# A graph network kernel: count matrices from steps of 256 edges instead of 128, and pair locations as bytes

## The reference: what is computed

```
# layer 0
h_proj = einsum('nd,rde->rne', h, relation_weight)
att = sum(h_proj[etype, src] * tanh(h_proj[etype, dst] + efeat), axis=-1)
a = softmax of att over the edges of each dst
h_nb = segment_sum(h[src] * a[:, None], dst)
# layer 1, four times
x = segment_sum(dinv[src] * dinv[dst] * x[src], dst)
# layer 2: gated convolution over (x[dst], x[src], edge_attr); layer 3: two attention layers
```

## Time and profile before

| | before |
|---|---|
| median of 3 runs | 9190.53 us (9164.67 to 9205.76) |
| the profiled execution | 9157.66 us, span 9156.1 us |
| mean granted TensorE clock | 0.608 |
| busy in the span | PE 3846.7 us (42%), DVE 5285.9 (58%), ACT 2454.3 (27%), POOL 3780.2 (41%) |
| count tiles' loads (tile<-adj) | 228 of 781.2 KB |
| x_src<-rows_s, window<-hpx in relation_rows | stores of 896 KB, loads of 256 KB |

### The profile page before, as it was taken

How to read it: one execution, slowest core, us unless ns; L and a number is a source line. 1 busy time by engine, 2 the same in 40 slices (tenths; PEclk the granted TensorE clock), 3 DMA queues, 4 the chain that set the end, 5 groups by cost and what they waited for, 6 DMA issues and landing times. The chain is left out here.

```text
span 9156.1 us, 102588 instructions
## 1 busy us (share of the span) xinstructions
PE 3846.7 (42%) x24601; PEld 3085.2 (34%) x24602; DVE 5285.9 (58%) x8989; ACT 2454.3 (27%) x3870; POOL 3780.2 (41%) x4315
## 2 busy tenths in 40 slices
PE   5455555520017881444443232222249522222196
PEld 2444444520017881333333210000048300000186
DVE  5454445569742112444444468888856588888675
ACT  4333333321622221433333221111112111111121
POOL 4444444400020004444444236666625166666261
PEclk8555555555558995666666555555579555555596
DMA  7565556677737881222222366666645477666462
GB/s 291 152 186 174 170 179 186 184 212 194 284 67 266 293 281 52 82 83 80 93 80 81 44 179 183 184 183 184 171 99 132 128 183 185 182 183 183 107 139 69
DMA packets 1551900, 1462.17 MB, mean 160 GB/s; under 512 B 1296593, under 2 KB 1344365, under 8 KB 1535296
## 3 DMA queue, kind: packets, MB, share of 16 engines
q1 hardware_dynamic: 966152, 807.40, 28.8%
q0 software_dynamic: 175712, 462.09, 19.3%
q10 hardware_dynamic: 409944, 191.70, 7.4%
HBM read 1078.30 MB, written 381.40 MB: 159 GB/s over the span
## 5 line engine op out<-in xcount | busy, mean ns | idle before, releaser
L2328 POOL DMA_INDIRECT rows_p<-node_rows,stage_i x1728 | 1637.9, 948 | 1090.7 <-issue 842.8
L2359 PE MATMUL psZ<-parts_r,hot_t 126*128 x1728 | 629.5, 468 | 1948.7 <-issue 966.3
L2359 PEld LDWEIGHTS psZ<-parts_r,hot_t 126*128 126x128 bf16 x1728 | 181.0, 105 | 2398.1 <-issue 2378.1
L715 PE MATMUL psP<-window,pair_hot 128*128 x3136 | 725.6, 420 | 579.4 <-issue 349.9
L790 DVE SCALAR_TENSOR_TENSOR pair_run<-pair_run,same_c,psP 128x64 f32<-128x64 f32 x1568 | 440.1, 281 | 871.9 <-remote 743.4
L2416 DVE TENSOR_TENSOR psZ<-psZ,rows_p 128x660 f32<-128x660 f32 x864 | 724.7, 846 | 357.7 <-issue 236.5
L715 PEld LDWEIGHTS psP<-window,pair_hot 128*128 128x128 f32 x3136 | 690.8, 329 | 626.7 <-issue 626.7
L257 POOL DMA_INDIRECT rows_s<-hpx,stage_i x784 | 748.5, 955 | 264.7 <-issue 242.7
L257 POOL DMA_INDIRECT both<-table,stage_i x784 | 742.9, 948 | 264.0 <-issue 242.6
L2423 DVE SCALAR_TENSOR_TENSOR lz<-psZ,att 128x660 f32<-128x660 f32 x864 | 723.0, 837 | 95.1 <-issue 69.1
L2429 DVE TENSOR_REDUCE sc<-lz 128x10 f32<-128x660 f32 x864 | 711.9, 831 | 59.4 <-issue 45.1
(11 more groups left out here) (523 smaller groups left out, 8016.2 us busy)
## 6 DMA issues: line engine op xcount, KB each, us to landing
tile<-adj SPq DMA_DIRECT2D x228, 781.2 KB, 4.8
x_src<-rows_p SPq DMA_DIRECT2D x288, 192.0 KB
xs<-x_src SPq DMA_DIRECT2D x432, 128.0 KB, 3.1
locs<-loc_rows SPq DMA_DIRECT2D x144, 378.0 KB
hpx<-stage ACTq DMA_DIRECT2D x25, 2048.0 KB
pair_loc<-pair_locs SPq DMA_DIRECT2D x28, 1792.0 KB
window<-hpx SPq DMA_DIRECT2D x196, 256.0 KB
dst_runs<-pair_run SPq DMA_DIRECT2D x28, 1792.0 KB
```

Source lines behind the costliest of these rows:

```text
L715: last = pe.matmul(psP[:, n % 2, j * D:(j + 1) * D], hot[:, n % 2, j * CE:(j + 1) * CE], window[:, n % 2, bass.ds(rel[j], 1), :].rearrange ...
L2328: pool.indirect_dma_start(rows[:, k, j, :], None, g.node_rows, bass.IndirectOffsetOnAxis(stage[:, k, j:j + 1], 0)).then_inc(got[k], 16)
L2359: last = pe.matmul(psZ[:, n % 4, j, 0:ZH], hot[:, k, col * CE:(col + 1) * CE], parts[:, bass.ds(at[col], 1), :].rearrange("p o c -> p (o c)"),
```

## The change

- A step is now CS = 256 edges, two chunks side by side (`e` = 0, 1): half as many chunks (CH = 392), fewer steps and NT = 42 tiles. `raw`, `place` and `quo` have 256 elements a step, `colsT` a further axis of 2; 10 rounds with 4 transposes and one copy.
- A step's counts are two matmuls that add in PSUM, each reading every second element of the one-hots. The one-hots of a tile are made in two units, of 12 and 13 steps (both written 13 wide, 6656 elements), with the iota in SBUF in 16 bits, each value twice side by side. The units follow batches 0, 3 and 5 of each chunk (`UNIT_AT`).
- A turn of two chunks makes 3 tiles, 21 parts over 14 batches (one and two in turn), with three tile buffers and a ring of 3 PSUM banks. PE waits for its own products behind both units of a tile. SP stores tiles at n = 2, 7 and 12. No tile is left behind the loops.
- The pair locations go through memory as bytes, one higher than before, and the lanes' number is one lower.

```diff
-CH = EP // CE
+CS = 2 * CE
+CH = EP // CS
 WD = 5
 NW = N // WD
 TS = 25
 TC = TS * WD
-NT = 57
+NT = 42
 S = NT * TS
-SP = 95
+SP = 105
...
+    g.colsT, g.iotaB = g.hot.sb("colsT", [P, 2, 2, S], bf16), g.hot.sb("iotaB", [P, P], bf16)
...
-        keys, locb = t.sb("keys", [CR, PT, CE], i32), t.sb("locb", [CR, PT, CE], bf16)
+        keys, locb = t.sb("keys", [CR, PT, CE], i32), t.sb("locb", [CR, PT, CE], u8)
...
-                        pool.indirect_dma_start(raw[:, n, q, :], None, a[name].rearrange("(c e) -> c e", e=CE),
+                        pool.indirect_dma_start(raw[:, n, q, :], None, a[name].rearrange("(c e) -> c e", e=CS),
...
-                    pe.transpose(psX[:, q % 2, 0:SP], quo[:, q, :], g.ident[0:SP, 0:SP])
-                    pe.transpose(psX[:, q % 2, P:P + SP], place[:, q, :], g.ident[0:SP, 0:SP]).then_inc(cols_turned, 1)
+                    for n, values in enumerate((quo, place)):
+                        for e in range(2):
+                            last = pe.transpose(psX[:, q % 2, (2 * n + e) * SP:(2 * n + e + 1) * SP],
+                                                values[:, q, e * CE:(e + 1) * CE], g.ident[0:SP, 0:SP])
+                    last.then_inc(cols_turned, 1)
...
-                c.link(v.tensor_tensor(locb[:, :, :], keys[:, :, :], pgroup[:, :].unsqueeze(2).to_broadcast([CR, PT, CE]), ALU.subtract))
-                c.link(v.tensor_scalar(locb[:, :, :], locb[:, :, :], -1.0, float(PN * R), ALU.max, ALU.min))
+                c.link(v.tensor_tensor(keys[:, :, :], keys[:, :, :], pgroup[:, :].unsqueeze(2).to_broadcast([CR, PT, CE]), ALU.subtract))
+                c.link(v.tensor_scalar(locb[:, :, :], keys[:, :, :], 0.0, float(PN * R + 1), ALU.max, ALU.min))
...
-                    v.tensor_copy(g.colsT[:, 0, q * SP:(q + 1) * SP], psX[:, q % 2, 0:SP])
-                    v.tensor_copy(g.colsT[:, 1, q * SP:(q + 1) * SP], psX[:, q % 2, P:P + SP]).then_inc(taken, 1)
+                    v.tensor_copy(g.colsT[:, :, :, q * SP:(q + 1) * SP].rearrange("p n e s -> p (n e) s"),
+                                  psX[:, q % 2, 0:4 * SP].rearrange("p (m s) -> p m s", m=4)).then_inc(taken, 1)
...
-    RING = 4
-
-    def __init__(self, nc, g, s):
-        self.nc, self.g = nc, g
-        self.cols = s.sb("cols", [P, 2, 2, TS], bf16)
-        self.hot = s.sb("hot", [P, 2, 2 * TS, P], bf16)
-        self.tile = s.sb("tile", [P, 2, NB, TC], bf16)
-        self.ps, self.iota = s.ps("psA", [P, self.RING, 512]), s.ps("ps_iota", [P, P])
-        self.hot_made, self.hot_used, self.stored = (
-            [s.sem(f"{n}{k}") for k in range(2)] for n in ("hot_made", "hot_used", "tile_stored"))
+    RING = 3
+    FIRST = 3
+    UNITS = (slice(0, FIRST * GS), slice(FIRST * GS, TS))
+    WIDE = TS - FIRST * GS
+
+    def __init__(self, nc, g, s, tiles):
+        self.nc, self.g, self.tiles = nc, g, tiles
+        self.cols = s.sb("cols", [P, 2, 2, self.WIDE, 2], bf16)
+        self.hot = s.sb("hot", [P, 2, 2 * self.WIDE, P, 2], bf16)
+        self.tile = s.sb("tile", [P, tiles, NB, TC], bf16)
+        self.iota = s.sb("iota_w", [P, P, 2], bf16)
+        self.ps = s.ps("psA", [P, self.RING, 512])
+        self.hot_made, self.hot_used = ([s.sem(f"{n}{k}") for k in range(2)] for n in ("hot_made", "hot_used"))
+        self.stored = [s.sem(f"tile_stored{k}") for k in range(tiles)]
         self.counted, self.moved = s.sem("counted"), s.sem("moved")
 
-    def one_hots(self, c, v, tile, k, turn):
-
-
-        v.wait_ge(self.hot_used[k], turn + 1)
-        at = bass.ds(tile * TS, TS) if not isinstance(tile, int) else slice(tile * TS, (tile + 1) * TS)
-        c.link(v.tensor_copy(self.cols[:, k], self.g.colsT[:, :, at]))
-        v.tensor_tensor(self.hot[:, k], self.cols[:, k].rearrange("p n s -> p (n s)").unsqueeze(2).to_broadcast([P, 2 * TS, P]),
-                        self.iota[:, :].unsqueeze(1).to_broadcast([P, 2 * TS, P]), ALU.is_equal).then_inc(self.hot_made[k], 1)
+    def one_hots(self, c, v, tile, k):
+
+
+        v.wait_ge(self.hot_used[k], tile + 1)
+        n, lo = self.UNITS[k].stop - self.UNITS[k].start, self.UNITS[k].start
+        at = bass.ds(tile * TS + lo, n) if not isinstance(tile, int) else slice(tile * TS + lo, tile * TS + lo + n)
+        c.link(v.tensor_copy(self.cols[:, k, :, 0:n, :], self.g.colsT[:, :, :, at].rearrange("p w e s -> p w s e")))
+        v.tensor_tensor(self.hot[:, k], self.cols[:, k].rearrange("p w s e -> p (w s) e").unsqueeze(2).to_broadcast([P, 2 * self.WIDE, P, 2]),
+                        self.iota[:, :, :].unsqueeze(1).to_broadcast([P, 2 * self.WIDE, P, 2]), ALU.is_equal
+                        ).then_inc(self.hot_made[k], 1)
 
     def dve_begin(self, c, v):
-        c.link(v.tensor_copy(self.iota[:, :], self.g.iotaB[:, :]))
+        c.mark(v.memset(self.cols[:, :, :, :, :], -1.0))
+        c.link(v.tensor_copy(self.iota[:, :, :], self.g.iotaB[:, :].unsqueeze(2).to_broadcast([P, P, 2])))
 
     def pe_begin(self, pe):
         for k in range(2):
             pe.sem_inc(self.hot_used[k], 1)
 
-    def products(self, pe, before, r, n, turn):
-
-        NG, GS, k = self.NG, self.GS, r % 2
-        if n == 0:
-            pe.wait_ge(self.hot_made[k], turn + 1)
-        pe.wait_ge(self.moved, before * NG + n + 1)
+    def products(self, pe, i, r, n):
+
+        NG, GS, k, tile = self.NG, self.GS, int(n >= self.FIRST), i * self.tiles + r
+        if n in (0, self.FIRST):
+            pe.wait_ge(self.hot_made[k], tile + 1)
+        pe.wait_ge(self.moved, tile * NG + n + 1)
         for j in range(min(GS, TS - n * GS)):
-            st = n * GS + j
-            last = pe.matmul(self.ps[:, (r * NG + n) % self.RING, j * TC:(j + 1) * TC], self.hot[:, k, st, :],
-                             self.hot[:, k, TS + st, 0:TC], start=True, stop=True)
+            st = n * GS + j - self.UNITS[k].start
+            for e in range(2):
+                last = pe.matmul(self.bank(r, n)[:, j * TC:(j + 1) * TC], self.hot[:, k, st, :, e],
+                                 self.hot[:, k, self.WIDE + st, 0:TC, e], start=e == 0, stop=e == 1)
         last.then_inc(self.counted, 1)
-        if n == NG - 1:
-            pe.wait_ge(self.counted, before * NG + NG)
+        if n in (self.FIRST - 1, NG - 1):
+            pe.wait_ge(self.counted, tile * NG + n + 1)
             pe.sem_inc(self.hot_used[k], 1)
+
+    def bank(self, r, n):
+        return self.ps[:, (r * self.NG + n) % self.RING]
 
     def act_begin(self, act):
         act.sem_inc(self.moved, self.RING)
-        for k in range(2):
+        for k in range(self.tiles):
             act.sem_inc(self.stored[k], 16)
 
-    def move(self, act, before, r, n, turn):
-
-        k, m = r % 2, min(self.GS, TS - n * self.GS)
+    def move(self, act, i, r, n):
+
+        tile, m = i * self.tiles + r, min(self.GS, TS - n * self.GS)
         if n == 0:
-            act.wait_ge(self.stored[k], turn * 16 + 16)
-        act.wait_ge(self.counted, before * self.NG + n + 1)
-        act.activation(self.tile[:, k, :, n * self.GS * WD:(n * self.GS + m) * WD],
-                       self.ps[:, (r * self.NG + n) % self.RING, 0:m * TC].rearrange("p (s a) -> p a s", a=NB),
-                       ACT.Copy).then_inc(self.moved, 1)
-
-    def store(self, sp, before, k):
-
-        sp.wait_ge(self.moved, before * self.NG + (self.NG + self.RING))
-        at = bass.ds(before * P, P) if not isinstance(before, int) else slice(before * P, (before + 1) * P)
-        sp.dma_start(self.g.adj[at, :], self.tile[:, k].rearrange("p a c -> p (a c)")).then_inc(self.stored[k], 16)
-
-    def sp_end(self, sp):
-        sp.wait_ge(self.stored[0], ((NT + 1) // 2 + 1) * 16)
-        sp.wait_ge(self.stored[1], (NT // 2 + 1) * 16)
+            act.wait_ge(self.stored[r], i * 16 + 16)
+        act.wait_ge(self.counted, tile * self.NG + n + 1)
+        act.activation(self.tile[:, r, :, n * self.GS * WD:(n * self.GS + m) * WD],
+                       self.bank(r, n)[:, 0:m * TC].rearrange("p (s a) -> p a s", a=NB), ACT.Copy).then_inc(self.moved, 1)
+
+    def store(self, sp, i, r):
+
+        tile = i * self.tiles + r
+        sp.wait_ge(self.moved, tile * self.NG + (self.NG + self.RING))
+        at = bass.ds(tile * P, P) if not isinstance(tile, int) else slice(tile * P, (tile + 1) * P)
+        sp.dma_start(self.g.adj[at, :], self.tile[:, r].rearrange("p a c -> p (a c)")).then_inc(self.stored[r], 16)
+
+    def sp_end(self, sp, turns):
+        for r in range(self.tiles):
+            sp.wait_ge(self.stored[r], (turns + 1) * 16)
...
-    TB = 4
-    assert M * BP * NCH == NP and 2 * Tiles.NG == 2 * M and TB * (NCH // 2) == NT - 1
+    TB = 3
+    UNIT_AT = {0: (0, 1), 3: (1, 0), 5: (1, 1), 7: (2, 0), 10: (2, 1), 12: (3, 0)}
+    parts_at = [[divmod(q, Tiles.NG) for q in range(TB * Tiles.NG * n // (2 * M), TB * Tiles.NG * (n + 1) // (2 * M))]
+                for n in range(2 * M)]
+    assert M * BP * NCH == NP and TB * (NCH // 2) == NT and TB * Tiles.NG % Tiles.RING == 0
```

(78 more changed lines are left out.)

4 lines of the change are left out of this document (2 added, 2 removed).

## The result

The changed kernel takes 8806 us (median of 4, 8788 to 8855) against 9187 us of the kernel before on the same chip: ratio 0.9595, 95% interval 0.9557 to 0.9634. That is faster by 381 us; forecast were 37 us (9187 or 9190 to 9150), and the range ended at 8985. The profiled execution took 8855.31 us, its span is 8853.0 us, 303 us shorter than the span of before.

The account below looks back on a forecast made before the run. PE bounds propagate; landing, gathers and tail set relation_rows' period. -153 - 5 + 3 + 119 - 4 = -40 us against the profiled 9157.7 gives 9118, or 9150 as a median; range 8985 to 9370.

Parts of the forecast that it names:

- What bounds the kernel: relation_rows chunk: landing some 11 us, gathers 35, tail 13; the crawl is single matmuls with idle between, beside running gathers.
- propagate: Four calls, PE-bound: 57 tiles become 42 in each, 60 fewer at 2.55 us, -153 us.
- Joins: TensorTensors of StepJoins: 1425 elements become 1050, about a dozen save about 0.4 us each, -5 us.
- first_tables: Count columns at its end: 15 rounds become 10 of about 1.1 us with twice the transposes, +3 us.
- One-hot at 3.6 us: relation_rows, DVE: each new 16 bit one-hot takes 3.6 us, 10.9 us a chunk instead of 13.6.
- Rival B: One-hots run no faster, 7.1 us, and hold POOL longer: +12 to +13 us a chunk, 9370 us; chance 0.14.
- One-hots hold POOL: relation_rows: a one-hot with both inputs in SBUF delays POOL's gathers by 0.87 of its length, +3.1 us for one inside.
- How many of them meet the gathers: Of three one-hots a chunk, one at the gathers' start (+1.0 us), one inside (+3.1), one with POOL idle (0).
- Tail (+0.3): From a chunk's last gather to the next store, 13 us: 4 to 8 more matmuls, one ACT move less, +0.3 us.
- rival A: Held gathers let PE catch up, tail 13.1 to about 8 us; chunk -2 to +1, centre 9030 us; chance 0.27.
- Rival C: More count products and PE's own waits lengthen the crawl: +3 to +5 us a chunk, about 9260 us; chance 0.16.
- The sum: Whole kernel: propagate, joins, first_tables, relation_rows chunks (+119 us) and the dropped last tile (-4) make -40 us.

Follow-up runs that it names:

- f1: Changed kernel with its 16 bit iota in PSUM, so one-hots don't hold POOL, on chip 7 with the crawl: 9228 us, 0.997 of the kernel before.
- h1: The changed kernel itself, unedited, measured again on chip 0 with the crawl: 9128 us, 0.979 of the kernel before there.
- a1: The changed kernel itself, unedited, measured again on chip 14 without the crawl: 7665 us, 0.996 of the kernel before there.
- b1: The kernel before itself, unedited, profiled again on chip 14 without the crawl: 7690 us.
- g1: Changed kernel with iota in PSUM and three own POOL stops of 2.4 us in each chunk's gathers, chip 0: 8696 us, 0.933 of before.
- e3: Kernel before with three own POOL stops of 2.4 us in each chunk's gathers, chip 4 without the crawl: 7787 us, 1.012.
- e1: Changed kernel with its 16 bit iota in PSUM instead of SBUF, chip 4 without the crawl: 7490 us, 0.974 of the kernel before.
- g3: Kernel before with six short POOL stops, one behind every fourth gather, each adding 1.15 us, chip 0: 8767 us, 0.941.
- g2: Kernel before with one POOL stop of 2.4 us behind the 14th gather of each chunk, chip 0: 9233 us, 0.991.
- e2: Kernel before with its fp32 iota in SBUF instead of PSUM, chip 4 without the crawl: 7947 us, 1.033.

## Why the prediction was wrong, point by point

- **What bounds the kernel**: right, in the three pieces landing, gathers, tail, and in seeing that the tail is PE's crawl. The tail was read as a fixed 13 us. It depends on how long POOL runs without a stop, and the trace of before had no stop to show it.
- **propagate**: -153 forecast, -138 measured. The term was mis-sized: I took 2.55 us a tile from the call's mean, with its waits in it. From one tile's first product to the next's it is 2.47 us in both kernels where nothing is waited for, so 60 tiles are -148, and PE's waits for tile loads rose over the four calls from 14.3 to 23.4 us, which takes 9 back.
- **Joins**: right. A TensorTensor of 2.75 us is now 2.06 (L1551, 1050 elements).
- **first_tables**: +3 forecast, about -5 measured. A round's one wide copy is 0.60 us rather than two of 0.25, and the rounds come 0.83 us apart instead of 1.1, so the ten take as long as the fifteen did. They don't set the start of relation_rows: its first product comes at 200.91 instead of 205.65 us, more than 10 us behind the last round in both kernels, and waits there for ACT's pair one-hots.
- **One-hot at 3.6 us**: right (3.63). Rival B is out. The lower bound in the prediction is 2.3 us (0.35 ns x 6656), not 2.5; nothing hung on it. The rule of the Trainium skill, "VectorE: DVE Perf Modes" (Mode 2×_1P), gave the value 3.6 too, and the trace agrees.
- **One-hots hold POOL**: right. The 51 gathers over 2 us of the kernel after last 3.77 us in the mean, at most 4.4, so a met one-hot costs POOL 2.8 us; forecast were 3.1. The 0.87 behind that was worked out with 1.6 us for the TensorTensor of the earlier trace rows, which shows 2.75, so its nearness is in part luck. With the iota in PSUM (f1) the gathers take 0.952 us. The Trainium skill's inference in "SBUF — State Buffer" (Who interferes with whom), that a TensorTensor doesn't hold DMA issue, doesn't hold here for 16 bit operands in SBUF either.
- **How many of them meet the gathers**: wrong. I counted one inside and one at the edge, from where DVE stood in the trace of before. With each stop the batches run on, so the next one-hot comes inside too, and three meet in the good chunks.
- **Tail (+0.3)**: the step that failed. In chunks with three stops there is no tail: the store comes within the gathers, and the period is theirs, 42.8 us. I had this as rival A with a chance of 0.27, and sized it by one batch: tail 13 to 8, a chunk -2 to +1. It was -5.6 us a chunk (60.3 to 54.7) and -17.5 in the mean of those with three stops, because with the tail gone the next gathers start at once.
- **Rival C**, longer work in the crawl: its price was about right, and hidden. f1 has no stops. On its own chip it is 31 us below the kernel before, and propagate gives 124 of it, so the rest costs some +93 us, +3.4 a chunk; against the first chip's period it is +5 (60.3 to 65.3). C had +3 to +5 above a gather that isn't held. Which of the longer products, the waits of PE for its own or the later moves makes it wasn't separated. As an estimate from runs on several chips, the change is then -124 to -138 (propagate), about +93 (longer work in the crawl), and -150 (h1) to -340 (first chip) by the stops, by how many meet.
- **The sum**: where nothing crawls it came out near: -31 us measured on a1, -40 forecast. That is partly luck. relation_rows grew by 121 us (1117 to 1238; forecast +119), but by gathers of 43.4 instead of 35.4 us a chunk, of which the 40.1 us period of b1 had room for a part: 80 gathers are held where I had counted about one a chunk and one at the edge.

## What to carry to other kernels

When an engine's slow stretch ends with another engine's run of DMA issues, don't take the slow stretch as a constant: something that breaks the run may remove it, and a cost on the path can come back several times over. Price both ends of such a loop, as the gain feeds itself (batches run on, the next stop comes in time) and so does the loss. If stops help, place them in the issuing engine's own program, every 4 to 9 issues, rather than leave them to where another engine's operations happen to fall: 0.933 with runs within 15 us of each other (g1, on one chip), against 0.9595 and 0.979 for the changed kernel, whose four runs beside g1 spread over 94 us. But find out first whether the slow stretch is there: on a chip without the crawl stops only cost (e3, 1.2%), and the kernel with none of them was the best (e1, 0.974).

## What the runs showed of the hardware that I had not expected

- Chips differ in this by 20%: the same kernel takes 7690 and 7697 us on two of them (4 and 14), 9259 and 9318 on two others (7 and 0), and 9187 on the first, which may be one of the latter two, with the granted clock of b1 (0.628) near that of before (0.608). Nearly all of the difference lies in relation_rows (1117 in b1 against 1697 us in before) and behind propagate (4827 against 5723). Behind propagate the same signs stand beside POOL's other gathers: PE waits 966 us in "issue" ahead of L2359 in before, and ACT 571 us for late semaphores at L1873, and b1 has neither wait; POOL's own idle time in "issue" ahead of the gathers of L2328 is 843 against 506 us. What in the chip causes it stays open.
- On a chip with the crawl, stops of 1.15 us behind every fourth gather, that is after 5 us of gathers, leave POOL no wait for the stores (g3, 0.1 us); one stop of 2.4 us in 35 us of gathers removes little (g2, 539 us of waits are left).
- A TensorTensor in 16 bits takes 3.62 us from PSUM (e1, f1) as from SBUF (3.63), and from PSUM it leaves POOL's gathers at 0.95 us.
- A gather beside a TensorTensor with two SBUF operands is held in 16 bits (after, up to 4.4 us beside one of 3.6) as with the fp32 iota (e2, up to 7.5 beside one of 6.8).
